# A fused two-layer gated cross-attention kernel: score products that contract two heads at a time, queries laid out by two masked copies, PSUM banks split by pair of heads

## The reference, cut to what matters

```
log_d = tril(cumsum(log_sigmoid(fg)) differences + ig)
m = max(log_d);  d = exp(log_d - m)
c = q @ (k.T / sqrt(dh)) * d
n = max(sum(c), exp(-m))
h = c / (n + eps) @ v
h = h * rsqrt(mean(h*h) + 1e-6) * (1 + rms_scale)
x = x + tanh(g) * h
```

## Time and profile before

| what | value |
|---|---|
| runs, us | 567.40, 564.77, 559.57 (median 564.77) |
| profiled execution | 559.68 us, of which 557.9 us are the span from first to last instruction |
| busy in the span | PE 86%, its weight loads 56%, DVE 59%, ACT 56%, POOL 35% |
| mean granted TensorE clock | 0.935 of full speed (2.4 GHz); it is granted at either 1.2 or 2.4 GHz |
| first pass | from the start to about 268 us |

### The profile page before, as it was taken

How to read it: one execution, slowest core, us unless ns; L and a number is a source line. 1 busy time by engine, 2 the same in 40 slices (tenths; PEclk the granted TensorE clock), 3 DMA queues, 4 the chain that set the end, 5 groups by cost and what they waited for, 6 DMA issues and landing times.

```text
span 557.9 us, 12799 instructions
## 1 busy us (share of the span) xinstructions
PE 477.2 (86%) x3767; PEld 312.4 (56%) x3767; DVE 326.7 (59%) x1442; ACT 315.0 (56%) x782; POOL 197.9 (35%) x208
## 2 busy tenths in 40 slices
PE   1699998788988898897879999999984887988995
PEld 1256656554555665564437777777742554655663
DVE  4435788787777777878423223322214576877774
ACT  4658777666766667522123333333304697888884
POOL 3401124444444444564600000000048887666200
PEclk9769999998889879999799999999995799999999
DMA  4965112222222101140131444433142355555422
GB/s 114 212 158 154 59 59 78 78 78 76 76 76 61 53 33 57 41 139 24 49 81 39 113 114 113 112 97 104 36 124 55 83 137 140 146 146 144 133 58 75
DMA packets 81483, 51.98 MB, mean 93 GB/s; under 512 B 7555, under 2 KB 74790, under 8 KB 81446
## 3 DMA queue, kind: packets, MB, share of 16 engines
q1 hardware_dynamic: 73766, 43.09, 28.5%
q0 software_dynamic: 7680, 8.43, 6.9%
HBM read 26.07 MB, written 16.91 MB: 77 GB/s over the span
## 4 chain that ended last, share of the span: by engine, by line
PE 56%; DVE 19%; issue 9%; ACT 8%; DMA 2%; POOL 2%; another core or an unknown queue 1%; DVEq 1%; ACTq 0%; SPq 0%; POOLq 0%
PE bank L1132 10%; PE heads L1125 10%; PE heads L1012 4%; PE heads L1022 4%; PE bank L1223 3%; PE heads L1037 3%; PE heads L1184 3%; DVE s_ln_stats L99 3%; ACT s_xn L151 2%; PE bank L985 2%; PE bank L978 2%; DVE s_cw L1349 2%; PE bank L979 2%; PE heads L1205 2%; PE heads L1180 2%
## 5 line engine op out<-in xcount | busy, mean ns | idle before, releaser
L720 POOL DMA_INDIRECT s_xs<-slots_y,s_gidx x32 | 49.9, 1560 | 148.5 <-DMA slots_y<-s_ye 131.3
L151 ACT ACTIVATE s_xn<-s_xs,s_ln_shift,s_ln_rstd 128x128 f32 (+1 forms) x192 | 77.7, 486 | 31.5 <-DVE s_ln_shift L144 31.1
L861 ACT ACTIVATE s_ht<-heads,s_cols 128x512 f32<-128x512 f32 x64 | 44.0, 687 | 80.6 <-PE heads L1125 80.3
L695 POOL DMA_INDIRECT slots_x<-s_xn,s_sidx x56 | 55.2, 985 | 64.4 <-DVE s_sidx L1437 51.6
L1132 PE MATMUL bank<-s_w_sb,s_ht 128*128 128x128 f32 x512 | 59.9, 275 | 0.9 <-DVE s_ye L1530 0.9
L1132 PEld LDWEIGHTS bank<-s_w_sb,s_ht 128*128 128x128 f32 x512 | 58.5, 192 | 1.5 <-issue 1.5
L1125 PE MATMUL heads<-s_xet,s_w_sb 128*128 128x512 f32 x128 | 57.8, 594 | 1.7 <-DVE s_xet L1521 1.7
L99 DVE BATCH_NORM_STATS2 s_ln_stats<-s_xs 128x6 f32 (+1 forms) x256 | 55.5, 280 | 4.7 <-issue 1.8
L682 POOL TENSOR_TENSOR s_hs<-s_hs,s_head_w 128x512 f32<-128x512 f32 x15 | 19.0, 1266 | 82.3 <-DVE s_hs L1387 82.2
L951 PE MATMUL bank<-s_ones_b 128*128 128x512 bf16 x156 | 42.5, 408 | 0.0
L1530 DVE TENSOR_TENSOR s_ye<-bank,s_b2b 128x512 f32<-128x512 f32 x16 | 11.1, 692 | 47.2 <-PE bank L1132 47.2
(11 more groups left out here) (199 smaller groups left out, 922.5 us busy)
## 6 DMA issues: line engine op xcount, KB each, us to landing
slots_x<-s_xe SPq DMA_DIRECT2D x8, 516.0 KB, 7.6
s_xe<-slots_x SPq DMA_DIRECT2D x16, 258.0 KB, 3.0
s_xs<-in_x_dram SPq DMA_DIRECT2D x16, 256.0 KB, 3.0
s_ctxb<-in_ctx_dram SPq DMA_DIRECT2D x16, 256.0 KB, 3.1
s_kpt<-s_kt SPq DMA_DIRECT2D x16, 256.0 KB, 2.4
s_w_sb<-in_L_ffn_w_dram SPq DMA_DIRECT2D x16, 256.0 KB
slots_y<-s_ye SPq DMA_DIRECT2D x16, 256.0 KB, 2.3
s_kpr<-s_kpt SPq DMA_DIRECT2D x16, 256.0 KB
```

The costliest lines, as they stand in the source:

```text
L151: last = act.activation(out(t), tile(t), ACT.Identity, bias=self.shift[:, j:j + 1], scale=self.rstd[:, j:j + 1])
L695: pool.indirect_dma_start(out=slots_x, out_offset=bass.IndirectOffsetOnAxis(ap=slots_of(g, q)[:, t:t + 1], axis=0), in_=routed(g)[:, q, t, ...
L720: pool.indirect_dma_start(out=xs[:, n * D:(n + 1) * D], out_offset=None, in_=slots_y, in_offset=rows_at, compute_op=ALU.add).then_inc(yg_i ...
L861: act.activation(ht[:, s_par, c, :], heads[:, c, :], ACT.Gelu_apprx_tanh, bias=col).then_inc(h_done, 1)
```

## The change

1. `queries_by_head` makes two copies instead of four. Copy j reads all 128 partitions of `bank[0]` and scales each by a column of a new constant `of_pair`, which is 1 where the partition's head has the parity j and 0 elsewhere. So for each sequence `qbd` has 2 x 64 columns: heads 0 and 2 share columns 0 to 63, heads 1 and 3 columns 64 to 127. The copies write the zeros themselves, and the memset of `qbd` on DVE is gone. POOL gets five small memsets for `of_pair`.
2. `scores` makes two products for each sequence, one for each pair of heads v (partitions 0 to 63 and 64 to 127): 64 partitions contracted, 64 keys wide, 128 columns. Pair v goes to bank v of `heads`. It counts `scores_done` up once for a group.
3. So the order of the 16 (tile, head) combinations becomes (pair, tile, head in pair) wherever they lie side by side: in `turn_gates` and `gate_values`, `cw`, `head_values`, `sq`, `hs`, and POOL's `add_heads`, whose two operations read and write the rows with a step.
4. Waits follow: `decayed_scores` waits for all scores of the group before its first half, `pv_done` counts two for a group.

```diff
-        cw = sb("cw", [P, GT, NH, S])
+        cw = sb("cw", [P, 2, GT, 2, S])
...
-        qbd = ht[:, :, :, :].rearrange("p q c n -> p q (c n)")
+        qbd = ht[:, :, 0:2, :].rearrange("p q c n -> p q (c n)").rearrange("p q (b j i) -> p q b j i", b=BG, j=2)
...
+            step(pool.memset(of_pair[:, :], 0.0))
+            for h in range(NH):
+                step(pool.memset(of_pair[h * HD:(h + 1) * HD, h % 2:h % 2 + 1], 1.0))
+            assert done == PAIR_AT
...
-                pool.tensor_tensor(hs[:, q, :, :], hs[:, q, :, :],
-                                   head_w[:, :].unsqueeze(1).to_broadcast([P, GT, D]), ALU.mult).then_inc(hsw_done, 1)
+                pool.tensor_tensor(hs[:, q, :, :, :], hs[:, q, :, :, :], head_weights_by_pair, ALU.mult).then_inc(hsw_done, 1)
...
-                pool.tensor_tensor(xgroup(g), xgroup(g), hs[:, q, :, :].rearrange("p t d -> p (t d)"),
-                                   ALU.add).then_inc(x1_done, 1)
+                pool.tensor_tensor(by_pair(g), by_pair(g), hs[:, q, :, :, :], ALU.add).then_inc(x1_done, 1)
...
-                need(act, scores_done, nth(g - 2, GT, GT))
+                need(act, scores_done, g - 1)
...
             def queries_by_head(g, half, q):
+
                 if isinstance(g, int) and g == 0:
-                    act.wait_ge(cleared, 4)
-                for h in range(NH):
-                    hp = slice(h * HD, (h + 1) * HD)
-                    act.activation(qbd[hp, q, :].rearrange("p (b h i) -> p b h i", b=BG, h=NH)[:, :, h, :],
-                                   bank[0][hp, :].rearrange("p (b i) -> p b i", b=BG), ACT.Copy).then_inc(qbd_done, 1)
+                    act.wait_ge(consts, PAIR_AT)
+                need(act, scores_done, g - 1)
+                for j in range(2):
+                    act.activation(qbd[:, q, :, j, :], bank[0][:, :].rearrange("p (b i) -> p b i", b=BG),
+                                   ACT.Identity, scale=of_pair[:, j:j + 1]).then_inc(qbd_done, 1)
...
             def scores(g, half, q):
 
+                hold(pe, qbd_done, nth(g, 2, 2), consts)
+                hold(pe, ex_done, g + 1, consts)
                 for t in range(GT):
-                    if t == 0:
-                        pe.wait_ge(qbd_done, nth(g, NH, NH))
-                        pe.wait_ge(ex_done, g + 1)
-                    for b in range(2 * t, 2 * t + 2):
-                        last = pe.matmul(heads[(b % 2) * S:(b % 2 + 1) * S, t // 2, (t % 2) * NH * S:(t % 2 + 1) * NH * S], kt[:, q, b * S:(b + 1) * S],
-                                         qbd[:, q, b * NH * S:(b + 1) * NH * S], start=True, stop=True)
-                    last.then_inc(scores_done, 1)
+                    for p in range(2):
+                        b = 2 * t + p
+                        for v in range(2):
+                            vp = slice(v * S, (v + 1) * S)
+                            last = pe.matmul(heads[p * S:(p + 1) * S, v, t * 2 * S:(t + 1) * 2 * S], kt[vp, q, b * S:(b + 1) * S],
+                                             qbd[vp, q, b, :, :].rearrange("p j i -> p (j i)"), start=True, stop=True)
+                last.then_inc(scores_done, 1)
...
-                dve.memset(qbd, 0.0).then_inc(cleared, 1)
...
                 if u == 0:
                     dve.wait_ge(ex_done, g + 1)
-                dve.wait_ge(scores_done, nth(g, 2 * u + 2, GT))
-                need(dve, pv_done, nth(g - 1, 2 * u + 2, GT))
+                    dve.wait_ge(scores_done, g + 1)
+                need(dve, pv_done, nth(g - 1, u + 1, 2))
```

More of the change, by code:

```diff
@@ L279, in flamingo @@
         zz = sb("zz", [P, 6, R])
-        hs = sb("hs", [P, 2, GT, D])
+        hs = sb("hs", [P, 2, 2, GT, D // 2])
         xn2 = sb("xn2", [P, 2, GT, D + 1])
@@ L442, in xgroup, with by_pair @@
             return xs[:, bass.ds(g * GW, GW)]
+        def by_pair(g):
+            return xgroup(g).rearrange("p (t v d) -> p v t d", t=GT, v=2)
+        head_weights_by_pair = head_w[:, :].rearrange("p (v d) -> p v d", v=2).unsqueeze(2).to_broadcast([P, 2, GT, D // 2])
         def routed(g):
@@ L792, in squares @@
                 need(act, ss_done, g)
-                act.activation(sq[:, :, :, :].rearrange("p (u t) h d -> p u (t h) d", u=2),
+                act.activation(sq[:, :, :].rearrange("p (u w) d -> p u w d", u=2),
                                heads[:, 2:4, 0:2 * NH * HA].rearrange("p u (w d) -> p u w d", d=HA)[:, :, :, 0:HD],
@@ L983, in turn_gates @@
                 pe.wait_ge(gate_rows_done, g + 1)
+                by_tile = bank[6][:, 0:2 * R].rearrange("p (w t j) -> p t w j", t=GT, j=2)
                 for t in range(GT):
-                    last = pe.matmul(bank[6][:, t * 2 * NH:(t + 1) * 2 * NH], gate_rows[:, t * P:(t + 1) * P],
-                                     ident[0:2 * NH, 0:2 * NH], start=True, stop=True)
+                    last = pe.matmul(by_tile[:, t, :, :], gate_rows[:, t * P:(t + 1) * P],
+                                     ident[0:2 * NH, 0:2 * NH].rearrange("p (w j) -> p w j", j=2), start=True, stop=True)
                 last.then_inc(gates_ps, 1)
@@ L1026, in head_values @@
             def head_values(g, half, q):
-                for t in range(GT):
-                    if t % 2 == 0:
-                        hold(pe, cw_done, nth(g, t // 2 + 1, 2), consts)
-                    if t == 0:
+                for v in range(2):
+                    hold(pe, cw_done, nth(g, v + 1, 2), consts)
+                    if v == 0:
                         pe.wait_ge(vaug_done, g + 1)
                         need(pe, hs_done, g)
-                    for h in range(NH):
-                        for b in range(2):
-                            bp = slice(b * S, (b + 1) * S)
-                            last = pe.matmul(heads[bp, 2 + t // 2, (t % 2 * NH + h) * HA:(t % 2 * NH + h + 1) * HA],
-                                             cw[bp, t, h, :], vaug[bp, q, t, h, :], start=True, stop=True)
+                    for t in range(GT):
+                        for j in range(2):
+                            for b in range(2):
+                                bp = slice(b * S, (b + 1) * S)
+                                last = pe.matmul(heads[bp, 2 + v, (t * 2 + j) * HA:(t * 2 + j + 1) * HA],
+                                                 cw[bp, v, t, j, :], vaug[bp, q, t, 2 * v + j, :], start=True, stop=True)
```

33 lines of the change are left out of this document (16 added, 17 removed).

## The result

| what | before | after |
|---|---|---|
| median of four runs, us | 562.89 (559.57 to 567.40) | 581.84 (578.23 to 582.69) |
| ratio | | 1.0299, 95% interval 1.0255 to 1.0344 |
| span of the profiled execution | 557.9 | 580.8 |
| mean granted clock, whole span | 0.935 | 0.876 |
| mean granted clock, window 55 to 245 us | 0.94 | 0.77 |

The forecast was 562 with a range of 552 to 569, so it failed: the time is outside the range, on the slower side. Of the 22.9 us by which the profiled execution is longer, 20.1 lie in the first pass. The experts behind it take the same time to a tenth.

A forecast was written before the change was run, and what follows sets the result against it. It took a 15.0 us ring of DVE and POOL, with the hold, to bound steps 8 to 17. 559.68 - 4.5 + 4 = 559.2 us for the profiled execution; relative to the 564.77 median it took 562, range 552 to 569.

The forecast's parts named there:

- The memset: At the start, removing DVE's 3.47 us memset lets the gate rows begin 2.4 us earlier, bounds 1.5 to 3.5.
- The score products: Four array corners at once make the scores 0.9 us shorter, worth 1.8 us in steps 3 and 4 together.
- The rest: ACT's shorter copies, POOL's stepped patterns, `gate_values` and the changed waits: nothing beyond the start, or at most 0.1 us a step.
- held steps: About ten steps, 8 to 17, in which POOL scatters and PE's results are announced late; the ring is 15.0 us long.
- the hold: What PE has finished is announced to others only about 0.9 to 1.0 us after POOL's fourth scatter DMA.
- The tail of 0.3 us: One score count in place of four starts ACT's key copy sooner: 0.3 us for all ten held steps, bounds 0 and 2.
- PE idle for longer before the gate products: Sign expected in the new profile's held steps: PE waits longer between its scores and the gate products; no size given.
- What it does to the clock: With thinner score work, between three and four more held steps lose PE's clock, 1.2 us each: 4 us more, ends 0 and 9.6.
- Rival (a): PE's score work is too short to affect the clock; only the 4.5 us gain remains, about 558 us; 25%.
- Rival (b): PE's late announcements follow slow scores, so 0.9 us more comes off each of ten steps: 546 to 551 us; 10%.
- Rival (c): The clock falls in all eight further held steps and in steps 5 to 7: 573 us, slower than before; 8%.
- Rival (d): Four corners don't run at once; scores stay 1.95 us, clock unchanged, only the start gains: about 560 us; 7%.

The follow-up runs named there:

- b_fill1: The kernel before the change, plus one 128x512 filler product of constants ahead of each group's scores: 568.21 us, ratio 1.0076.
- b_masked: The kernel before the change with only the memset of `qbd` removed, using four masked copies over all 128 partitions: 561.10 us, ratio 0.9979.
- c_k128: The changed kernel with its 32 score instructions each contracting over all 128 partitions, not 64: 562.82 us, ratio 1.0016.
- a_fill1: The changed kernel plus one 128x512 filler product of constants ahead of each group's scores: 562.65 us, ratio 1.0001.
- a_three: a_fill1 with three indirect DMAs for a group's scatter in place of four, the fourth tile's rows left out: 546.08 us in one execution.
- a_late1: The changed kernel with a 128x512 filler product ahead of the scores only from step 5 on: 559.04 us, ratio 0.9957.

## Why the prediction was wrong, step by step

**The memset: right at the gate rows, not shown behind them.** 2.4 us at the gate rows were forecast and 2.7 came. With the memset they begin at 19.76 and, in b_fill1, at 19.40; in the twelve profiles without it at 16.61 to 17.05. That the first scores came 3.3 us sooner is another matter. b_fill1 has the same instructions as the kernel before up to there, ran them at the full clock, and its PE was at the filler ahead of the first scores at 34.70, 3.6 us sooner than the scores of the kernel before and sooner than in every profile without the memset (34.88 to 37.16). So an execution differs from the next by as much as this term, and how much of it reaches the scores isn't shown.

**The score products: right.** Four corners at once, 1.10 us, 0.83 us off each of steps 3 and 4 (10.16 against 10.99). The forecast for the two terms was 4.2 us and the lead at step 5 was 4.9; that these lie so close is in part luck, by the paragraph above.

**The rest: right, but for one small thing.** Copies, patterns and waits cost nothing (b_masked, c_k128). Of the ten held steps that I had counted, eight (8 to 15) are as long as the hold makes them; 16 and 17 took 13.3 and 11.4 us before the change. The tail of 0.3 us that one count in place of four should give became a loss of about 0.4 us in each held step, since the last score instructions don't get issued in the hold. I had assumed that PE gets through all of its scores there. For the same reason the sign "PE idle for longer before the gate products" didn't come: in step 9 the idle pieces are 1.01 and 0.77 us, together less than the 1.94 of before.

**What it does to the clock: the right mechanism for four of five long falls, and the term that failed, the price of a fall.** I had written that more of the eight held steps would lose the clock, at 1.2 us each, 3.3 of them: 4 us. The number of steps was of the right kind: five became long, and the other seven together stayed as they were. But the price was taken from one kind of fall only, that of the earlier trace rows, in which the gate products alone ran at half speed and the clock was back for what followed. After the change the clock stays low through most of a long step, for 10 to 17 us at a time. So the sentence that low clock in the second half of a step costs little, true of the single falls before, failed with it. Then it doubles everything on PE in it: gate products +1.7 us, value products 2.06 to 3.63, turned gates 1.05 to 1.87. That is 1.70 + 1.57 + 0.82 = 4.1 us, with 0.4 for the late key copy 4.5; less PE's 0.35 of slack it is 4.2 a step, and four of the five long steps are 19.4 to 20.2 us, the fifth 17.7, against 15.1. The five together are 21.2 us above five of 15.1, three and a half times my price for each. The twelve steps sum to 25.0 us more, the start and the scores gave 4.9 back, and the first expert product is 20.1 late.

The rule that I had cited, of the Trainium skill (TensorE: Matmul & The Clock Gate, HAM oscillation), says that each return of the clock is paid again, and that held. What it names as the cause are waits between bursts, of several microseconds in its example; here PE's longest single idle pieces before the falls in steps 11, 13 and 15 are 1.2 to 1.4 us (3.2 in step 7), and in step 9 PE's only idle pieces from 112.6 us to the fall at 116.0 are 0.56 and 0.14 us. So most of the falls here don't follow the example of the skill, and what exactly brings the clock down stays open. And through the low stretch PE is in work for 12.23 of 13.00 us without getting its clock back.

**Rival (a), the clock doesn't care:** refuted by a_fill1. **Rival (b), the hold follows the scores:** refuted; DVE's reduction stays 0.98 to 1.27 us behind the fourth scatter in all nine steps though the scores became shorter, and a_three makes the steps shorter with the scatter. **Rival (c), the clock falls in nearly every step:** it had 8% and 573 us, and of the four its sign was right; it had the same price of 1.2 us in it, so that even all its steps gave too little. (By its own figures it would have decided from the fourth additional fall and not the fifth, since 4 x 1.2 = 4.8 is already more than 4.5.) **Rival (d), corners not at once:** refuted by 1.10 us.

What I should have done: ask of the earlier trace rows not only what the fall did cost there, but what stands behind it on PE in a step whose bound PE is within 0.35 us of. The worst case of the term, half speed for a whole step, could be worked out from the rows of before: gate products, value products and turned gates are 1.88 + 2.06 + 1.05 = 5.0 us of PE's work between the release and `gate_values`, done twice, so up to 4.6 us a step behind the 0.35 of slack. It was no bound of my range, and should have been.

## What to carry to other kernels

Work of TensorE that is hidden behind a wait isn't free to remove when the wait itself can't shorten: the clock may pay for it, and then it is the work behind the wait that gets slower, all of it. Before shortening such a stretch, price a whole step at 1.2 GHz, and try the shortened version once with a filler product in the same place; if that wins the time back and the granted clock returns with it, it was the clock. And when a cheaper form wins only at the edges (here 10.16 us in steps 3 and 4), use a filler only where its cost lies under another engine's work, as a_late1 does.

## What the runs showed of the hardware

- Score products in the four 64 x 64 corners run together: 1.10 us for 32 instructions of 128 columns, against 1.59 when neighbours share the row half, and 1.99 when they contract over all 128 rows.
- A low clock may last: 13 us at 0.50 with PE in work for 12.23, in the changed kernel.
- With a filler of 1.0 us over all 128 rows the median clock over the whole span was 0.939 with 128 columns of the array and 0.937 with 64; with 64 rows it was 0.924.
- The clock differs between executions of the same instructions: 0.50 from 20.8 to 37.9 us in the kernel before, 1.00 over that stretch in b_fill1, and PE at its scores 3.6 us sooner there.
- While POOL issues its four indirect DMAs, what PE has finished reaches DVE only 0.8 to 1.3 us behind the end of the fourth (three exceptions above). In eight of nine such steps of the changed kernel PE itself stood after 26 to 29 of its 32 score instructions, until about the release.
- A scatter less (a_three) takes 1.1 us off each held step: the hold, and not PE or DVE, sets the step when the clock is good.
